# Moving the computation of the routed rows' places, and the sending of those rows, to later steps of a fused attention and mixture-of-experts kernel

## What is computed

```python
xn = layernorm(x)
# branch s: block-sparse attention, 16 heads of 16, blocks of 32 keys
gate = einsum(q, block means of k); idx = top_k(gate, 4)      # the block choice
mask = (chosen blocks) & causal
s = rmsnorm(softmax(where(mask, q @ k.T / 4, -1e30)) @ v) @ Wo.T
# branch g: mixture of experts, 8 experts of width 176, the best 2 of each token
scores = softmax(xn @ gate_w); topk_w, topk_idx = top_k(scores, 2)
routed = sum over the 2 chosen experts of topk_w * (silu(xn @ w_gate) * (xn @ w_up)) @ w_down
shared = (silu(xn @ sw_gate) * (xn @ sw_up)) @ sw_down        # width 352, all tokens
g = routed + shared
```

## Time and profile before

| | |
|---|---|
| median of 3 runs | 406.1 us (405.85 to 408.53) |
| the profiled execution | 409.56 us, its span in the trace 407.7 us |
| mean granted clock of TensorE | 0.908 |
| busy | PE 313.8, DVE 279.1, ACT 164.7, POOL 122.7 us |
| layer 0 | 0 to about 303 us; the changed region is 53 to 130 us |

### The profile page before, as it was taken

The page is one execution under the profiler, slowest core; times in us unless marked ns, Lnnn a source line. Parts: engine busy times, 40 slices in busy tenths (PEclk is TensorE's granted clock), DMA queues, the critical chain, the costliest instruction groups (busy, mean ns, idle before and its releaser), DMA issues. The chain is left out here.

```text
span 407.7 us, 5771 instructions
## 1 busy us (share of the span) xinstructions
PE 313.8 (77%) x1762; PEld 203.5 (50%) x1762; DVE 279.1 (68%) x865; ACT 164.7 (40%) x332; POOL 122.7 (30%) x105
## 2 busy tenths in 40 slices
PE   0699638567578799899899999994625998995981
PEld 0487527455344455555555555542614784444741
DVE  3857799986489778777234444447839969378694
ACT  1413611451012223232665656562303676938510
POOL 2555545577002111111113434445145000000123
PEclk9999897988588899999999999999685898998898
DMA  8992377456998374755443424015017000000011
GB/s 276 307 287 62 103 166 213 128 149 229 247 183 175 105 178 115 207 161 149 111 143 93 127 77 118 0 29 181 0 33 240 0 2 0 0 0 2 0 51 51
DMA packets 52545, 47.88 MB, mean 117 GB/s; under 512 B 5282, under 2 KB 50204, under 8 KB 52509
## 3 DMA queue, kind: packets, MB, share of 16 engines
q1 hardware_dynamic: 50211, 42.12, 38.7%
q0 software_dynamic: 1872, 4.22, 3.0%
q10 hardware_dynamic: 432, 1.18, 1.0%
HBM read 35.44 MB, written 15.87 MB: 126 GB/s over the span
## 5 line engine op out<-in xcount | busy, mean ns | idle before, releaser
L501 POOL DMA_INDIRECT yt_dram<-ysb,x x23 | 23.0, 1001 | 117.5 <-ACT ysb L617 78.9
L673 ACT ACTIVATE PT<-bank 128x512 f32<-128x512 f32 (+1 forms) x88 | 44.9, 559 | 21.5 <-PE bank L1177 20.8
L889 DVE TENSOR_REDUCE mx<-bank 128x1 f32<-128x384 f32 (+3 forms) x88 | 52.2, 636 | 1.5 <-PE bank L1159 0.8
L1158 PE MATMUL bank<-KS,QS 112*128 112x128 bf16 (+3 forms) x128 | 34.9, 319 | 12.3 <-DVE mx L889 10.7
L1788 PE MATMUL lbank<-u,w_ai 128*128 128x512 f32 x72 | 33.0, 619 | 1.9 <-issue 1.9
L1176 PE MATMUL bank<-QS,KS 115*128 115x512 bf16 (+3 forms) x128 | 31.0, 302 | 2.7 <-ACT PT L673 1.1
L1491 POOL TENSOR_TENSOR left<-xn,x 128x256 f32<-128x256 f32 x8 | 6.9, 897 | 85.9 <-DVE xn L1718 85.9
L1032 DVE SCALAR_TENSOR_TENSOR s<-th,bank 128x176 f32<-128x176 f32 x23 | 7.7, 336 | 33.7 <-ACT th L705 33.6
L507 POOL TENSOR_TENSOR small<-small,mhalf 128x16 f32<-128x16 f32 x8 | 24.4, 3046 | 17.3 <-DVE small L935 17.3
L1158 PEld LDWEIGHTS bank<-KS,QS 112*128 112x128 bf16 x128 | 12.7, 100 | 31.0 <-DVE mx L889 26.5
L1159 PE MATMUL bank<-tri,ident_b 128*128 128x128 bf16 x128 | 25.6, 227 | 0.0
(11 more groups left out here) (280 smaller groups left out, 807.8 us busy)
## 6 DMA issues: line engine op xcount, KB each, us to landing
wr<-w_dram SPq DMA_DIRECT2D x12, 352.0 KB
wt<-w_dram SPq DMA_DIRECT2D x11, 352.0 KB
QS<-parts_dram SPq DMA_DIRECT2D x12, 256.0 KB
KS<-parts_dram SPq DMA_DIRECT2D x12, 256.0 KB, 5.2
xs_dram<-x SPq DMA_DIRECT2D x1, 2967.0 KB, 15.4
x<-xs_dram SPq DMA_DIRECT2D x23, 129.0 KB, 2.8
w_dram<-in_w_chunks_dram SPq DMA_DIRECT2D x11, 256.0 KB, 4.8
wr<-in_w_chunks_dram SPq DMA_DIRECT2D x12, 176.0 KB
```

What stands on the lines that cost most here:

```text
L501: pool.indirect_dma_start(yt_dram, bass.IndirectOffsetOnAxis(ap=xg[:, n % XBUF, D:D + 1].bitcast(I32), axis=0), ysb[:, n % 2, :], None, bo ...
L673: act.activation(PT[:, k % 8, 0:n], bank[k % 2][:, 0:n], ACT.Exp, scale=float(DH) ** -0.5).then_inc(P_ready, 1)
L889: dve.tensor_reduce(mx[:, b * TB + i, heads[0]:heads[-1] + 1], bank[k % 2][:, 0:len(heads) * n].rearrange("p (h n) -> p h n", n=n), AX.X, ...
L1158: pe.matmul(out, QS[0:R_MAX, b, h, i * P:(i + 1) * P], KS[0:R_MAX, b, h, 0:n], start=True, stop=False)
```

## The change

Three things move; no instruction is added or removed.

- `expert_places` moves on DVE from the end of step 0 to the end of step 2, behind slot 11, which is the last of the block choice of batch 0.
- The sends of choice 0 move on POOL from four each in steps 1 and 2 to all eight at the end of step 3; those of choice 1 from four each in steps 3 and 4 to all eight at the end of step 4.
- `second_choice` moves on DVE from behind the first slot of step 3 to the end of step 3, behind `take_y(0)`.

```diff
+PLACE_STEP, SEND_STEP = 2, [3, 4]
@@ POOL
-                if 1 <= s <= 4:
-                    k = (s - 1) // 2
-                    if s == 1:
+                for k in range(EK):
+                    if s == SEND_STEP[k]:
                         pool.wait_ge(pad_in, 16)
-                    pool.wait_ge(routed, LABELLED[k])
-                    for t in range((s - 1) % 2 * TB, (s - 1) % 2 * TB + TB):
-                        send_rows(k, t)
+                        pool.wait_ge(routed, LABELLED[k])
+                        for t in range(T):
+                            send_rows(k, t)
@@ DVE
-                if s == SCH:
-                    second_choice()
                 for q in qs[1:]:
                     slot(q)
-                if s == 0:
+                if s == PLACE_STEP:
                     expert_places()
                 if s == SCH:
                     take_y(0)
+                if s == SEND_STEP[1] - 1:
+                    second_choice()
```

## The result

The changed kernel takes 412.61 us (median of 4 runs, 412.22 to 414.65) against 407.31 (405.85 to 409.06) for the one before, timed in the same rounds: ratio 1.0166, 95% interval 1.0123 to 1.0210. It is slower, by 6.7 us if the ratio is applied to the median that stood ahead of the prediction. The forecast was 12.5 us (418.6). All ratios here leave out runs more than 1.5% above the fastest run of the same kernel.

The account below looks back on a forecast made before the run. No engine is full; waits before about 130 us decide, then PE's pace. Part 1 at 0 plus 12.5 us of delay, added to the 406.1 us median, gave 418.6 us, range 414.0 to 422.5.

Parts of the forecast that it names:

- the weights of tile 2 bind, not the gather: At tile 2 PE waits for weights, a bound of 13.3 us, against 10.1 us from the first gather.
- the delay reaches the end of layer 0 whole: Behind tile 2 all runs in order at PE's pace, so the 12.5 us delay reaches the end whole.
- Part 1: Places moved behind the block choice on DVE: still 6.5 us, gain zero, loss 0.4 us.
- Part 3: On DVE, second_choice waits for step 3's sends: a 12 us stall, then 1.1 us of its own before step 4.
- What the delay costs PE: Late rows at PE: gather bound 10.1 us, tile 2's weights bound 13.3 us; 12.5 us taken.
- let 0.8 go: At tile 2, allowance of 0.8 us for transfers no longer colliding with the QS loads, giving 12.5 us.
- 13.3: SP issues the rows at 116.5 instead of 103.17, 13.3 us later; tile 2's weights move with them.
- The second: Sends on POOL lose their 0.30 us gaps beside idle DVE, 4.2 us less: 8.3 us, 414.4; chance 0.05.
- The first rival: At tile 2 the weights don't bind; only the gather's bound stays: 10.1 us, 416.2; chance 0.2.
- The third (the clock): Long wait at tile 2 halves PE's clock, up to 3 us more: 15.5 us, 421.6; chance 0.15.
- The fourth: Rows don't wait for sends if the sixteenth starts by 100.2: 406.1, or up to 1.1 us faster; chance 0.04.

Follow-up runs that it names:

- e5: Kernel before, with POOL's layer-1 weight split waiting until DVE has normed all eight tiles; 405.26 us, ratio 0.9955 to before.
- e6: Changed kernel, with POOL's layer-1 weight split waiting until DVE has normed all tiles; 414.28 us, ratio 1.0141 to the kernel before.
- e1: Changed kernel with the places back at the end of step 0; 417.79 us, ratio 1.0255 to the kernel before.
- e9: Kernel before, with POOL's split of the third chunk held until the places are done; 405.43 us, ratio 0.9936.
- e8: Kernel before with places in step 1, layer-1 split held behind the norms, batch 1's QS loads behind tile 3's weights; 402.86 us, ratio 0.9870.

## Why the prediction was half right

- **Right:** the sends of choice 0 at the end of step 3, one each 1.28 us (9.1 us from first to last, forecast 9.0); landed 2.0 us after their end (forecast 2.0); DVE stalled for 11.0 us (12) and with it everything of step 4; `gl` 2.2 us behind the start of step 4 (2.1); the weights of tile 2 bind, not the gather; the delay reaches the end of layer 0 whole in the first pair of profiles (in that of e5 and e6 it grows by 2.3 us).
- **Part 1, priced at +0.4, is the first failed step.** "They take DVE from 53.87 to 60.39, 6.5 us" was taken as the cost at the new place too. It was 4.0: 2.5 of the 6.5 us were a collision with POOL that the trace showed in the lengths of two instructions (e1, e9). A gain that the prediction excluded, of 2.4 us. The bias copy did stay behind `gh` of step 3 and came with it at 78.42.
- **Part 3, the term of `second_choice`,** 1.1 us, has the same fault: its first instruction takes 0.18 us when POOL is idle (96.58), not the 1.03 of the earlier trace rows, which ends with POOL's instruction beside it (82.14 and 82.10). Step 4 starts 0.2 us behind the landing, not 1.1. POOL in the kernel before:

```profile
80.95 1.15 POOL L518 TENSOR_TENSOR wp<-rot_a,wp 128x512 bf16<-128x512 f32 x1 [1.81 <-ACT wp L656]
```

- With the run's own offset of 0.6 us (everything up to 53 us is that much earlier, in unchanged code) these make 3.9 of the 4.2 us by which the last send starts earlier, at 109.38 instead of 113.6; with a landing of 1.6 in place of 2.0 the rows are issued at 111.93 instead of 116.5: 4.6 us.
- **"What the delay costs PE" is the second failed step.** From the rows' issue to PE's use of tile 2's weights 24.6 us were carried over; it took 21.9 (111.93 to 133.83). The reason given, that SP's queue and the KS load make that span, was wrong for its middle: between the rows and the KS loads stands a wait for parts to land, and it is shorter without the QS loads. SP's queue in the kernel before:

```profile
105.23 2.93 SPq L418 DMA_DIRECT2D parts_dram<-KS  x6
...
112.21 3.83 SPq L431 DMA_DIRECT2D KS<-parts_dram  x6
```

From the issue of the parts to that of KS it was 7.0 us; in the changed kernel it is 4.3 (113.72 to 118.04), and in e8, where the QS loads stand behind, 4.6 (102.33 to 106.97). That is the whole 2.7 us; I had let 0.8 go.
- The account closes, 13.3 - 4.6 - 2.7 = 6.0 against 6.05 at tile 2, but by construction: each term is a measured row set against its forecast, and 0.6 of the 4.6 is the offset of one execution, not an effect of the change.
- **The rivals.** The second, faster sends beside an idle DVE, didn't show: while DVE stood idle the pitch was 1.28 us with the same 0.30 ahead of each. The effect that the Trainium skill warns of there doesn't show between a DVE that is idle and one full of MAX8 and MATCH_REPLACE8; whether these are instructions that it means no run here tells. The lock on the shared port of the same section, which I didn't apply to DVE's own instructions, was the one that counted. The first rival (the weights don't bind) is out: tile 2 waited 1.57 us for its weights. The third (the clock) came in part: the granted clock was 0.60 from 130 to 132 and 0.50, the lower of its two levels (1.2 GHz), from 132 to 136, around that wait, but what it costs is not set apart from the rest (see e6). The fourth is out: the sixteenth send started at 109.38, not by 100.2, and SP waited for it.
- **Left open:** whether the change costs the 6 us of the first pair of profiles or the 8 of the second (the timed ratios give 6.7 and 7.5), how much of that is the clock behind tile 2, and what spreads the runs of one kernel over 3 to 4 us beside layer 1's collision.

## What to carry to other kernels

Before a block of instructions is moved, hold each duration in it against the same operation elsewhere in the trace: one that takes ten times as long as its size asks is waiting, and that cost stays behind when the block moves. A long idle time in front of a wait is not its price; what the wait holds up has to be late on the path that sets the end, and here POOL's queue of sends kept the rows 5.9 us late without it (109.02 against 103.17), where with it they were 8.8 late. A landing time read at one point holds only for the traffic at that point: 1.6 us on nearly empty DMA engines, 4.4 and 6.5 behind six loads of 256 KB.

## What the hardware showed that was not expected

- A small DVE instruction that runs beside a POOL instruction that reads SBUF can stand until that one ends: a scan of 8 elements 1.77 us against 0.17, a comparison of 184 elements 1.25 against 0.35, an int32 copy of 8 elements 1.03 against 0.18, and in layer 1 one norm of 256 elements 3.6 us against 0.40, beside a POOL split of 3.42. Only for the first two and the norms was POOL's work moved away by itself (e9, e5). Not all are stopped: in the kernel before, the MATCH_REPLACE8 from 72.90 to 74.11 take their usual 0.16 to 0.17 us beside POOL's `gl` (72.87 to 74.16).
- Whether the norm meets POOL's split hangs on 1 us: the weights landed 4.4 us after their issue in the kernel before and 5.5 in the changed one. Two profiles that are 6 us apart at the start of layer 1 then differ by 3 at its end.
- An indirect send of 128 rows occupies POOL for 0.97 us with 0.30 between two (the first of a group up to 1.16), whether DVE is idle or full. Its landing took 1.5 to 6.5 us, by the traffic of the DMA engines.
